# Second and third cross-attention: keys projected to the heads' 8 channels, scores of four heads from one product

## The reference, cut to what matters

```
x = x + L0_xattn(ln(x), ctx);  x = x + L0_ffn(ln(x))        # mixture of 8 experts
# L1
Q = (x @ Wq.T) as 16 heads x 8;  K, V = (ctx @ Wkv.T) as 16 heads x 8 each
attn = softmax(Q K^T * 8**-0.5);  x = x + (attn V) @ Wo.T
x = x + int8-quantized product (x @ rhs)
# L2: the same attention with biases bq, bk, bv, bo; then a Fourier-domain product
# L3: self-attention, a cross-attention to the normalized context, an MLP; a block-sparse FFN
```

## Time and profile before

| | |
|---|---|
| runs of the kernel | 4040.52, 4043.03, 4044.92 us; median 4043.03 |
| profiled execution, span from first to last instruction | 4037.7 us |
| what lies around the span, against the median | 5.3 us |
| mean granted TensorE clock | 0.954 of full speed |
| busy over the whole span | PE 94%, DVE 78%, ACT 66%, POOL 63%, weight load 71% |
| chain that ended last | PE 87%, DVE 6%, POOL 2%, ACT 2%, DMA 1% |

### The profile page before, as it was taken

The page is one execution under the profiler, slowest core; times in us unless marked ns, Lnnn a source line. Parts: engine busy times, 40 slices in busy tenths (PEclk is TensorE's granted clock), DMA queues, the critical chain, the costliest instruction groups (busy, mean ns, idle before and its releaser), DMA issues.

```text
span 4037.7 us, 110587 instructions
## 1 busy us (share of the span) xinstructions
PE 3793.1 (94%) x43467; PEld 2886.6 (71%) x43467; DVE 3135.7 (78%) x6499; ACT 2674.0 (66%) x5365; POOL 2544.9 (63%) x2457
## 2 busy tenths in 40 slices
PE   6999999989969999999799999996997899999987
PEld 4777777766637777777577777775765677777765
DVE  6999999858978888888577888886654788888864
ACT  4888887756637777777467777773442577777752
POOL 4888888759856776767456676675001476676761
PEclk8999999979989999999699999998998899999988
DMA  4333333125432222121112212110000212122100
GB/s 129 104 110 112 110 108 107 41 92 158 143 100 61 57 60 61 54 61 49 28 54 62 59 54 64 57 54 21 3 1 18 64 54 64 57 59 61 55 22 15
DMA packets 157328, 266.80 MB, mean 66 GB/s; under 512 B 26632, under 2 KB 97432, under 8 KB 155432
## 3 DMA queue, kind: packets, MB, share of 16 engines
q1 hardware_dynamic: 156360, 259.67, 22.5%
q10 hardware_dynamic: 448, 0.06, 0.0%
HBM read 165.10 MB, written 50.26 MB: 53 GB/s over the span
## 4 chain that ended last, share of the span: by engine, by line
PE 87%; DVE 6%; POOL 2%; ACT 2%; DMA 1%; issue 1%; SPq 1%; POOLq 0%; DVEq 0%; ACTq 0%
PE ps L186 83%; PE ps L659 1%; DVE xn L166 1%; POOL wst L539 1%; PE ps L242 1%; PE ps L255 1%; PE ps L1638 1%; DVE wst L817 1%; DVE wst L772 0%; PE ps L1160 0%; DVE st L151 0%; DMA big<-big 0%; DVE relu L769 0%; DMA ynN<-cx 0%; ACT wb L324 0%
## 5 line engine op out<-in xcount | busy, mean ns | idle before, releaser
L539 POOL TENSOR_TENSOR wst<-wst 125x384 bf16<-125x384 f32 (+1 forms) x1536 | 1432.0, 932 | 843.4 <-ACT wst L745 783.1
L745 ACT ACTIVATE wst<-ps 125x448 f32<-125x448 f32 x3072 | 1518.5, 553 | 569.3 <-PE ps L186 554.8
L186 PE MATMUL ps<-big,cx 128*125 128x448 bf16 (+1 forms) x6144 | 1428.8, 354 | 0.8 <-DMA big<-topT 0.8
L186 PEld LDWEIGHTS ps<-cx,wst 125*128 125x128 bf16 x23040 | 1113.5, 98 | 307.5 <-POOL wst L539 15.2
L817 DVE TENSOR_TENSOR wst<-wst 125x512 bf16<-125x512 f32 (+1 forms) x1536 | 1269.4, 827 | 56.8 <-ACT wst L745 56.5
L186 PE MATMUL ps<-cx,wst 125*128 125x65 bf16 (+2 forms) x23040 | 1202.4, 204 | 12.1 <-POOL wst L539 11.6
L186 PEld LDWEIGHTS ps<-big,cx 128*125 128x125 bf16 (+1 forms) x6144 | 835.1, 137 | 284.2 <-issue 1.8
L186 PE MATMUL ps<-cx,big 128*128 128x500 bf16 (+1 forms) x2688 | 709.4, 317 | 10.2 <-DVE big L1743 2.6
L772 DVE TENSOR_REDUCE wst<-ps 128x1 f32<-128x500 f32 x896 | 603.9, 674 | 136.6 <-PE ps L186 123.9
L769 DVE CUSTOM_DVE_ANT_0 wst<-ps,wst 128x500 bf16<-128x500 f32 x448 | 302.6, 676 | 207.2 <-PE ps L186 150.8
L769 DVE CUSTOM_DVE_ANT_0 relu<-ps,relu 128x500 bf16<-128x500 f32 x448 | 301.8, 674 | 147.8 <-PE ps L186 84.1
(11 more groups left out here) (250 smaller groups left out, 4260.2 us busy)
## 6 DMA issues: line engine op xcount, KB each, us to landing
big<-big SPq DMA_DIRECT2D x768, 56.0 KB, 2.7
cx<-ctxT SPq DMA_DIRECT2D x96, 375.0 KB, 3.5
cx<-ctxN SPq DMA_DIRECT2D x64, 377.9 KB
cx<-in_ctxN SPq DMA_DIRECT2D x64, 375.0 KB
cx<-ctxT SPq DMA_DIRECT2D x96, 187.5 KB, 3.8
ctxN<-cx SPq DMA_DIRECT2D x32, 377.9 KB
ynN<-cx SPq DMA_DIRECT2D x32, 377.9 KB
cx<-ynN SPq DMA_DIRECT2D x32, 377.9 KB
```

Source lines behind the costliest of these rows:

```text
L186: return t.matmul(o, l, r, start=start, stop=stop, skip_group_check=True)
L539: g.tensor_tensor(pl[r][0:KP, at:], pf[r][0:KP, at:], pf[r][0:KP, at:].bitcast(BF16)[:, 1::2], ALU.subtract).then_inc(s["plp"], 1)
L745: e.activation(pf[T % 3][0:KP, cols], bank(2 + n2 % 3, 448)[0:KP], ACT.Exp, scale=scale).then_inc(s["ev"], 1)
```

## The change

Passes 1 and 2 get functions of their own: `sp_head`, `pe_head`, `act_head`, `dve_head`. Passes 0 and 3 stay as they are. For each element PE projects the 64 context channels into the 128 head channels (`pe_keys`, three chunks of 500 columns, two products each); ACT copies the high part (`act_keys`), DVE subtracts for the low part (`dve_keys`), both in the same turn; SP stores both to DRAM scratch (`kD`) and loads them back as `Ks`: 32 rows of high, 32 of low and 32 of high for each group of four heads, and row 96 of ones. Queries are projected for a pair of elements at once into 128 channels, split, stored to DRAM (`qD`, zeroed at the start) in a block-diagonal order, and loaded as `Qm` (128 rows, for the maxima) and `Qs` (97 rows, for the scores). A turn's scores are then four products of 224 columns, one for each group of heads. The products for the maxima keep number and size, with `KH` in the place of `cs`. The folding of query and key weights and the bias rows fall away. The split of `pf - high(pf)` moves from 512 to 448 columns for DVE.

```diff
-JP = (5, 4, 4, 4)
+SPLIT = (640, 448, 448, 512)
 def pe_fold(t, w, f, n, nd, wq, wk, wv, wo, weights, value):
-            for j in range(H // per):
+            for j in range(0 if f in EARLY else H // per):
...
 def act_fold(e, w, f, n):
-            for j in range(1 if f == 3 else 0, H // per, 2 if f == 3 else 1):
+            if f in EARLY:
+                w.wait_ge(s["w"], (0, 224, 336)[f])
+                e.activation(wqh, wqs[:, 0:128], ACT.Copy).then_inc(s["f1a"], 1)
+                e.activation(wkh, wks, ACT.Copy).then_inc(s["f1a"], 1)
...
+        KEY_SLOT = {21: (4, 0), 1: (2, 1), 4: (2, 2), 8: (3, 0), 12: (3, 1), 16: (3, 2)}
+        def head_slot(T):
+            p, i = divmod(T, 24)
+            for later, name in ((0, "keys"), (1, "keys split")):
+                if i - later in KEY_SLOT:
+                    more, c = KEY_SLOT[i - later]
+                    return (name, 2 * p + more, c) if 1 <= 2 * p + more < B else ("", 0, 0)
+            if i == 23 and 1 <= p + 2 < NP:
+                return "query", p + 2, 0
+            if i == 0 and 1 <= p + 1 < NP:
+                return "query split", p + 1, 0
+            if 1 <= p <= NP and i in (6, 7, 14, 15):
+                return ("turn", "turned")[i % 2], p - 1, 2 * p - 2 + (i >= 14)
+            if 1 <= p <= NP and i in (18, 19, 20):
+                return ("out 0", "out 1", "add")[i - 18], p - 1, 0
+        def sp_head(y, w, ci):
+            for T in range(-44, NT):
+                if (k := due(T, -44)) >= 0:
...
+                    y.dma_start(cs[i], cT2[k]).then_inc(s[f"lT_{i}"], 16)
+                if (k := due(T, -18)) >= 0:
...
+                    y.dma_start(kD[u, 0], KH[u]).then_inc(s[f"stT_{u}"], 16)
+                    w.wait_ge(s["pd"], projected_low(ci, "keys", k, 2))
+                    y.dma_start(kD[u, 1], KL[u]).then_inc(s[f"stT_{u}"], 16)
...
+                    w.wait_ge(s["pa"], projected(ci, "query", m))
+                    for v, of in enumerate((qhb, qlb)):
+                        for r in range(2):
+                            y.dma_start(diagonal(qD[2 * (m % 2) + r, v]), of[m % 2][:, 64 * r:64 * r + NQ]).then_inc(s[f"qd_{m % 2}"], 16)
+                        w.wait_ge(s["pd"], projected_low(ci, "query", m))
+                if (k := 0 if T == -44 else due(T, -22) or -1) >= 0:
+                    wait_query_stored(w, ci, k // 2)
...
+                    y.dma_start(Qm[k % 2], rows_of(qD[k % 4, 0])).then_inc(s[f"ql_{k % 2}"], 16)
+                if (k := due(T, -14)) >= 0:
...
+                    for n, v in enumerate((0, 0, 1)):
+                        y.dma_start(Qs[k % 3][32 * n:32 * n + 32, :].rearrange("r (g c) -> r g c", g=4),
+                                    grouped(qD[k % 4, v])).then_inc(s[f"lx_{k % 2}"], 16)
+                if (k := due(T, -11)) >= 0:
+                    wait_keys_stored(w, ci, k)
...
+                    for n, v in enumerate((0, 1, 0)):
+                        y.dma_start(Ks[u][32 * n:32 * n + 32, :, 0:M], by_group(kD[u, v])).then_inc(s[f"lx_{u}"], 16)
...
+        def pe_keys(t, w, ci, k, c):
+            wait_keys(w, ci, k)
+            o, of = bank(keys_bank(k, c), 500), cs[k % 3][:, 500 * c:500 * c + 500]
+            mm(t, o, wkh, of, True, False)
+            mm(t, o, wkl, of, False, True).then_inc(s["pm"], 1)
+        def act_keys(e, w, ci, k, c):
...
+            e.activation(KH[u][:, 500 * c:500 * c + 500], bank(keys_bank(k, c), 500), ACT.Copy).then_inc(s["pa"], 1)
+        def dve_keys(v, w, ci, k, c):
...
+            v.tensor_tensor(KL[u][:, cols], bank(keys_bank(k, c), 500), KH[u][:, cols], ALU.subtract).then_inc(s["pd"], 1)
+        def pe_head(t, w, ci):
...
+                    for hf in range(2):
+                        w.wait_ge(s["ev"], evac + n2 - 2)
+                        for g in (2 * hf, 2 * hf + 1):
+                            at = 4 * NQ * g
+                            r = mm(t, bank(2 + n2 % 3)[:, at - 448 * hf:at - 448 * hf + 4 * NQ],
+                                   Ks[u][0:97, g, KP * i:KP * i + 128], Qs[k % 3][0:97, at:at + 4 * NQ], True, True)
+                        r.then_inc(s["sc"], 1)
...
 def sp_l0(y, w):
             load_fold(y, s["w"], "L0", 64, 64)
+            w.wait_ge(s["idb"], 4)
+            for k in range(4):
+                for v in range(2):
+                    y.dma_start(rows_of(qD[k, v]), rowb[:, 0:HQ // 2].bitcast(BF16)).then_inc(s[f"qd_{k % 2}"], 16)
...
 def pe_l1(t, w):
             wait_f0(w)
+            for c in range(3):
+                pe_keys(t, w, 1, 0, c)
             pe_turn(t, w, xn, s["xn"], 32, 1)
...
 def pe_f1(t, w):
-            for h in range(H):
-                k, at = 2 * (h // 8), 64 * (h % 8)
-                i = mm(t, bank(k)[0:1, at:at + 64], bqv[:, 0, h:h + 1], wk[0:8, h, :], True, True)
-            i.then_inc(s["qbm"], 1)
...
 @block.sync
-            wait_stored(w)
             wait_split(w)
-            sp_cross(y, w, 1, cN2, cT2)
+            sp_head(y, w, 1)
             sp_f1(y, w)
-            wait_f1(w)
-            sp_cross(y, w, 2, cN2, cT2)
+            sp_head(y, w, 2)
```

More of the change, by code:

```diff
@@ L26 @@
 RND = 12582912.0
+ONES = 1.0 + 127 / 65536
 class Gate:
@@ new lines, in build, with projected, projected_low @@
+        HEAD_LAST = 24 * NP + 21
+        PROJECTED = [("keys", 0, 0), ("keys", 0, 1), ("keys", 0, 2), ("query", 0, 0)] + [
+            head_slot(T) for T in range(-26, HEAD_LAST) if head_slot(T)[0] in ("keys", "query")]
+        def projected(ci, what, p, c=0):
+            return projections(ci) + PROJECTED.index((what, p, c)) + 1
+        def projected_low(ci, what, p, c=0):
+            n = projected(ci, what, p, c)
+            return n if p else projections(ci) + (1 if what == "query" else c + 2)
@@ new lines, in act_head, with query, relu @@
+        def act_head(e, w, ci):
+            t0, b0 = NT * ci, B * ci
+            def query(p):
+                w.wait_ge(s["pm"], projected(ci, "query", p))
+                if p >= 2:
+                    wait_query_stored(w, ci, p - 2)
+                if ci == 2:
+                    e.activation(qhb[p % 2], bank(7, 128), ACT.Identity, bias=wqs[:, 128:129]).then_inc(s["pa"], 1)
+                else:
+                    e.activation(qhb[p % 2], bank(7, 128), ACT.Copy).then_inc(s["pa"], 1)
+            def relu(k, item):
+                kb = b0 + k
+                w.wait_ge(s["mxm"], products_to(kb, item) + 1)
+                n, j = halves(kb, item), int(item[1])
+                w.wait_ge(s["red"], maxima(kb, f"s{j - 2}") + 1 if j >= 2 else maxima(kb - 1, f"s{j + NJ - 2}") + 1)
+                e.activation(relus[n % 2], bank(max_bank(kb, k, item), 500), ACT.Relu).then_inc(s["half"], 1)
+            query(0)
+            w.wait_ge(s["zo"], zeroed(ci))
+            n2 = 0
+            for T in range(-26, HEAD_LAST):
+                if (k := due(T, -4)) >= 0:
+                    w.wait_ge(s["rw"], b0 + k + 1)
+                    w.wait_ge(s[f"tops_{k % 2}"], 16 * (ci * B // 2 + k // 2))
+                    e.activation(topT[k % 2][:, :], bank(2 + n2 % 3, 128)[0:NJ], ACT.Copy).then_inc(s["ev"], 1)
+                    n2 += 1
+                if (k := due(T, KT + 2)) >= 0:
+                    kb = b0 + k
+                    w.wait_ge(s["pv"], KT * (kb + 1))
+                    if k >= 2:
+                        w.wait_ge(s["fp"], 4 * (kb - 1))
+                    whole = raw[k % 2].rearrange("p j c -> p (j c)")
+                    e.activation(whole[:, 0:452], ps[:, 2620:3072], ACT.Copy).then_inc(s["fc"], 1)
+                    e.activation(whole[:, 452:], ps[:, 3072:2620 + 129 * NJ], ACT.Copy).then_inc(s["fc"], 1)
+                what, p, k = head_slot(T)
+                if what == "keys split":
+                    act_keys(e, w, ci, p, k)
+                if what == "query split":
+                    query(p)
+                if what == "turned":
+                    w.wait_ge(s["otr"], b0 + k + 1)
+                    if p >= 2:
+                        w.wait_ge(s["om"], NP * ci + p - 1)
+                    r = k % 2
+                    e.activation(ob[p % 2][:, :, 64 * r:64 * r + NQ], bank(7).bitcast(BF16)[:, 0:HQ].rearrange("c (h q) -> c h q", h=H),
+                                 ACT.Copy).then_inc(s["oc"], 1)
+                for k, items in turns(T):
+                    if items[0][0:1] == "d":
+                        relu(k, items[0])
+                if 0 <= T < NT:
+                    for hf in range(2):
+                        cols = slice(448 * hf, 448 * hf + 448)
+                        w.wait_ge(s["sc"], 2 * (t0 + T) + hf + 1)
+                        if T >= 3:
+                            w.wait_ge(s["pv"], t0 + T - 2)
+                        e.activation(pf[T % 3][0:KP, cols], bank(2 + n2 % 3, 448)[0:KP], ACT.Exp, scale=8 ** -0.5).then_inc(s["ev"], 1)
+                        n2 += 1
+                for k, items in turns(T):
+                    if items[1][0:1] == "d":
```

(5 more changed lines are left out.)

386 lines of the change are left out of this document (313 added, 73 removed).

## The result

| | median us (lowest to highest) | against before |
|---|---|---|
| before | 4042.36 (4040.52 to 4044.92, 4 runs) | |
| after | 4113.26 (4111.92 to 4114.67, 4 runs) | 1.0177 [1.0165, 1.0189] |

The forecast was 3899 us, range 3805 to 3985: 214 us too low, and on the wrong side of no change. The span of the profiled execution went from 4037.7 to 4112.3 us, +74.6.

The account below looks back on a forecast made before the run. PE bounds passes 1 and 2; after the change four engines stand in one band at 20.7 us an element. Span 4037.7 - 66.3 (pass 1) - 72.5 (pass 2) - 5 (boundaries) = 3893.9, plus 5.3: 3899 us, range 3805 to 3985.

Parts of the forecast that it names:

- PE's prices: Passes 1 and 2: four score products 0.385 us for 0.77, key products 0.21 each, weight loads hidden; PE 18.93 us an element.
- The pace: Steady turns of passes 1 and 2: 20.7 us an element for 22.84 and 23.04, bounds 19.1 and 22.0.
- DVE's wait: Three key turns of an element: DVE may wait 0.6 us each for ACT's copy, 1.8 at most; 0.5 taken.
- DVE's lengths: Passes 1 and 2: DVE's work, from the earlier trace's lengths, goes from 18.55 to 19.3 us an element.
- the POOL rival: Passes 1 and 2: POOL becomes the bound, its operation 1.22 for 0.83 us beside DVE's; 22.0 us an element, 3980 us; 25%.
- The 6% for the chain: Passes 1 and 2: PE idles 6%, as in pass 1's last turns before, so 18.93/0.94 = 20.2 us an element.
- The boundaries: Outside the steady turns: start +1.5, before pass 1 +5, before the experts -7, before pass 2 -5; sum taken as -5 us.
- the queries' trip: Query split, four stores, landing, `Qm` load through DRAM: some 9 to 11 us of the 11 that 7 turns leave; hidden in the mean.
- The rivals: For the whole kernel: PE stays the bound, 3800 us (15%); POOL becomes it, 3980 (25%); slower by late queries, 4085 (6%).
- "slower": Whole kernel slower than before, 7%; of it 6% for queries late through DRAM, PE standing once in two elements, 4085 us.

Follow-up runs that it names:

- POOL narrow: Changed kernel with POOL's part of the subtraction 32 columns wide in place of 448 in passes 1 and 2, from the fourth turn on: 4003.24 us, 0.9907 of before.
- Late: Changed kernel with DVE's low parts of keys and queries a turn after ACT's copy, nothing else moved: 3987.30 us, 0.9865 of before.
- late with POOL narrow: Changed kernel with DVE's low parts a turn later and POOL's part of the subtraction 32 columns wide: 3914.50 us, 0.9681 of before.
- Runs 3 and 6: Kernel before, passes 1 and 2: score products cut from 448 to 224 columns, 3928.30 us; the same with POOL's part 32 columns wide, 3881.49 us.
- run 1: Changed kernel with DVE's low parts of keys and queries at the head of the next turn, nothing else moved: 3987.30 us, 0.9865 of before.

## Why the prediction was wrong

**PE's prices: right.** Four score products take 0.38 us from start to start, as predicted from the earlier trace rows; the value products keep 0.61:

```profile
1499.39 0.55 PE L207 MATMUL ps<-big 97*128 97x224 bf16 x4
1499.77 0.38 PE L207 MATMUL ps<-diff,big 128*128 128x500 bf16 x1
1499.99 0.78 PE L207 MATMUL ps<-cx,wst 125*128 125x129 bf16 x15
1500.60 0.38 PE L207 MATMUL ps<-cTs,big 128*128 128x500 bf16 x1
```

The two products of a key chunk take 0.43 (1509.36 to 1509.79), as priced. Four weight loads don't hold four products of 224 columns up. The clock was 1.00, DMA share 0.49 and 127 GB/s for the 150 expected at the faster pace.

**The pace: wrong.** All the error is in the 20.7 us an element: it was 24.24, above my upper bound of 22.0 too.

**DVE's wait: the step that failed first.** "DVE ... may wait for one copy (0.6 us) each time, 1.8 at most; ... I take 0.5." Measured: 44.4/400 x 24.24 = 2.7 us an element, above my upper bound. The bound was wrong in kind. I priced the wait by the length of the copy (587 ns here), as if ACT and DVE came to the turn together; it is set by how far ACT's list is behind DVE's, up to 1.83 us. Without it the pace is 1.9 us better, where I had put 0.5. And the engine that PE stood for was DVE; I had taken the loss from turns in which PE waits for POOL, and in this window it never did.

**DVE's lengths: the second.** Undisturbed, my sum was right: with POOL narrow DVE works 334.1/400 x 22.7 = 19.0 us an element, for 19.3 predicted. In the changed kernel it works 345.0/400 x 24.24 = 20.9. I took the 770 ns of the earlier trace rows with its disturbance as fixed, though it belongs to a PE-bound loop in which POOL cost DVE only 0.4 us an element. Late less late with POOL narrow: 22.31 - 21.31 = 1.0 us of pace. I had the contention in my text, under the POOL rival, and priced only POOL's side of it. POOL's mean came to 1.03 us, below my 1.05 to 1.15, and POOL is 67% busy: not the bound by its own work. This timeline of the changed kernel shows both sides:

```profile
1346.08 3.22 POOL L585 TENSOR_TENSOR wst<-wst 125x448 bf16<-125x448 f32 x3
...
1347.16 1.34 DVE L1236 TENSOR_TENSOR wst<-wst 125x448 bf16<-125x448 f32 x1
1348.42 1.15 DVE L1204 TENSOR_TENSOR diff<-cTs 128x500 bf16<-128x500 bf16 x1
...
1348.56 0.79 PE L207 MATMUL ps<-cx,wst 125*128 125x129 bf16 x15 [1.43 <-DVE wst L1236]
```

Through POOL's three subtractions, DVE needs 1.34 us for one that takes 0.61 elsewhere, and PE stands 1.43 us for it.

**The 6% for the chain: too small.** With both costs off, the pace is 21.3 us for PE's 18.9: 11% lost, against the 6% that I read from the last turns of the earlier trace rows. (PE's busy share of 95% hides part of this, since it counts the latency of each product.) Runs 3 and 6 on the kernel before show the same (20.7 at best). The terms together: 20.7 + 1.4 (wait, 1.9 for 0.5) + 1.0 (contention) + 1.1 (chain, 21.3 for 20.2) = 24.2. The sum closes because each term is a difference of two of these runs; in another order the shares are others (POOL narrow first: 1.6). What makes up the last term was not taken apart: the waits that are left are many and short, for DVE, ACT and PE in turn.

**The boundaries: right in their sum.** -6.0 for -5. At the start the first fold began 2.2 us later and lasted 6.6 us for 4.3 before, at a granted clock of 0.54 for 0.83; the last `top` of pass 0 comes 3.4 us later (772.9 for 769.5; +1.5 predicted). The expert stage's value fold, with line 274, begins at 818.38, for line 255 at 822.97 before: -4.6 so far, so -8.0 since that `top` (-7). The first `top` is 1.6 us earlier (1205.4 for 1207.0), so the entry of pass 1 took +3.0 of these back (+5). From there the queries' trip and the first product for the maxima can be read in the timeline:

```profile
1184.96 3.16 SPq L960 DMA_DIRECT2D headq<-wa  x4
...
1189.40 0.35 SPq L966 DMA_DIRECT2D big<-headq  x1
...
1192.18 0.57 PE L207 MATMUL ps<-diff,big 128*128 128x500 bf16 x1 [7.60 <-DMA big<-headq]
```

PE starts at 1192.18, not at my 1199 to 1200. The first load had landed at 1176.8, where I had 1182. Of the four stores only the two of the high part went out beside the addition to x (1184.44 to 1186.73); the two of the low part came behind it, as I had it. From the end of the addition, stores, landing and `Qm` took 5.4 us of the 8 that I gave them. The first `top` gained less than the start of PE did, 1.6 us: 13.2 us lie between them, for 10.9 before. Between the passes -5.1 (-5), after the last `top` +0.7 (0).

**The rivals.** None of mine was this. I gave "slower" 7%, 6% of it to the queries' trip, which cost nothing that can be measured: from the first `top` of a pass on PE waited for it once, for the second element (2.5 and 2.7 us), and not again up to the last. My sum of 9 to 11 us for that trip leaves out the landing at its end; with it, it would have been 12 to 13, later than the 11 there are; the trip was quicker than either sum. The wait for ACT stood in my sum as a small term and not among the rivals, although I wrote that DVE had no room for all of it.

The Trainium skill ("SBUF — State Buffer", "Who interferes with whom") says that a VectorE instruction with two SBUF inputs contends with a GpSimd instruction that reads SBUF, that the shared pair of ports is an exclusive lock, and that a reduction never takes part. By that rule lines 1236 and 1204 suffer, and the operations on PSUM don't. The trace agrees on who: 831 for 718 ns and 1145 for 413 with POOL wide, 668 to 680 ns for the PSUM readers in both. Whether it is a lock, no run here shows.

## What to carry to other kernels

Count the waits of an in-order engine as its work: 86% busy with 11% spent on one wait is a full engine, and a new wait must be priced by how far the other engine's list is behind, not by the operation waited for. Place the consumer of another engine's fresh result in the middle of the turn or a turn later; here one move of a few lines made 4113 us into 3978. When the bound of a loop goes away, lengths of VectorE operations with two SBUF inputs read beside a busy GpSimd no longer hold: price them from minimum to minimum plus the neighbour's operation (line 1236: 607 to 1347 ns, beside operations of 1033 in the mean).

## What the runs showed of the hardware that was not expected

- One subtraction of 500 bf16 columns on VectorE took 1143 to 1146 ns in all 17 cases of the changed kernel between 1300 and 1700 us and 411 to 415 ns in all 17 with GpSimd narrow: a contention can be as regular as a fixed length. With the low parts a turn later (run 1) it took 561 to 732.
- Contention depends on the phase of two lists. The same instructions and shapes, at a pace of 21.2 for 22.8 us an element, went from 773 to 881 ns and from 408 to 1040 ns.
- Five more transfers of 384 KB an element beside a TensorE at 100% changed the time by no more than 0.1%.
